# Attention scores on a head's own rows: K kept once, two units' products interleaved on two groups of rows and two banks

## What is computed

```
layer 0:  q,k of 64 per head, v of 16;  scores = (q + r_w) k^T + shifted((q + r_r) r^T);  softmax;  @ v;  @ Wo
layer 1:  q,k,v of 16 per head;          scores = q k^T / 4;   softmax;  @ v;  @ Wo     (after a gated convolution)
layer 2:  q,k,v of 64 per head;          scores = q k^T / 8;   softmax;  @ v;  @ Wo
```

## Time and profile before

| | |
|---|---|
| three runs | 1695.86, 1707.94, 1713.18 us |
| median | 1707.94 us |
| span of the profiled execution (first to last instruction) | 1698.1 us |
| median less this span | 9.8 us |
| PE busy, share of the span | 1444.5 us, 85% |
| ACT busy | 662.5 us, 39% |
| DVE busy | 683.9 us, 40% |
| POOL busy | 384.9 us, 23% |
| chain that ended last, by engine | PE 58%, issue 12%, DVE 12%, DMA 8%, ACT 6% |

### The profile page before, as it was taken

The page is one execution under the profiler, slowest core; times in us unless marked ns, Lnnn a source line. Parts: engine busy times, 40 slices in busy tenths (PEclk is TensorE's granted clock), DMA queues, the critical chain, the costliest instruction groups (busy, mean ns, idle before and its releaser), DMA issues.

```text
span 1698.1 us, 31669 instructions
## 1 busy us (share of the span) xinstructions
PE 1444.5 (85%) x10300; PEld 1049.9 (62%) x10300; DVE 683.9 (40%) x2124; ACT 662.5 (39%) x2237; POOL 384.9 (23%) x464
## 2 busy tenths in 40 slices
PE   5899986796756778888899899699999999989994
PEld 3666664632212345666678799466765776789994
DVE  5557766511101376444423622433542423551113
ACT  1667663410000233777842122153663632213331
POOL 5212222300000122222200266220220200123441
PEclk8899996587778688999998899799999999889997
DMA  8434341679998400000003366200000200126553
GB/s 219 133 83 129 82 115 28 227 242 333 311 314 249 147 1 1 1 0 0 0 0 100 107 203 197 81 1 1 0 0 0 93 37 0 30 84 199 181 175 103
DMA packets 94439, 178.73 MB, mean 105 GB/s; under 512 B 35578, under 2 KB 54168, under 8 KB 92704
## 3 DMA queue, kind: packets, MB, share of 16 engines
q1 hardware_dynamic: 80144, 130.65, 26.1%
q10 hardware_dynamic: 7056, 30.67, 5.6%
q0 software_dynamic: 7136, 16.10, 3.1%
HBM read 150.39 MB, written 26.99 MB: 104 GB/s over the span
## 4 chain that ended last, share of the span: by engine, by line
PE 58%; issue 12%; DVE 12%; DMA 8%; ACT 6%; SPq 3%; POOL 1%; DVEq 0%; ACTq 0%; POOLq 0%
PE bank L1819 15%; DMA WM<-in_fc 7%; PE bank L2339 6%; PE bank L2325 4%; PE bank L1910 4%; PE bank L1922 3%; PE bank L1939 3%; PE bank L2329 3%; PE bank L1949 3%; PE bank L2000 2%; PE bank L1885 2%; PE bank L1992 2%; ACT ON L1604 2%; SPq L226 2%; PE bank L2256 1%
## 5 line engine op out<-in xcount | busy, mean ns | idle before, releaser
L1819 PE MATMUL bank<-XT,AREA 96*128 96x408 f32 (+1 forms) x640 | 239.1, 532 | 33.9 <-ACT XT L1558 16.6
L1819 PEld LDWEIGHTS bank<-XT,AREA 96*128 96x128 f32 (+1 forms) x640 | 122.1, 196 | 139.8 <-issue 99.8
L1910 PE MATMUL bank<-KZ,QT 128*102 128x102 f32 x1152 | 140.8, 262 | 9.0 <-ACT PB L1604 5.7
L664 POOL TENSOR_TENSOR PB<-PB,RCU 102x306 f32<-102x306 f32 x96 | 69.2, 720 | 318.5 <-DVE RCU L923 318.4
L648 POOL TENSOR_TENSOR RS<-VE,expo 102x4 f32<-102x4 f32 (+1 forms) x53 | 53.0, 1001 | 387.2 <-DVE VE L863 329.8
L1910 PEld LDWEIGHTS bank<-KZ,QT 128*102 128x102 f32 x1152 | 122.4, 174 | 27.2 <-issue 18.1
L2339 PE MATMUL bank<-WM,KZ 128*128 x660 | 118.2, 327 | 0.0
L2339 PEld LDWEIGHTS bank<-WM,KZ 128*128 128x128 f32 x660 | 105.7, 190 | 0.4
L1585 ACT ACTIVATE KZ<-bank,AREA 128x128 f32<-128x128 f32 x198 | 54.6, 374 | 121.8 <-PE bank L2329 121.8
L1922 PE MATMUL bank<-AREA,OT 128*102 128x192 f32 x384 | 88.9, 345 | 11.3 <-DVE SLOTS L1276 5.3
L1939 PE MATMUL bank<-PT,V 102*32 102x102 f32 (+1 forms) x1152 | 85.9, 270 | 14.5 <-DVE OT L933 12.3
(11 more groups left out here) (335 smaller groups left out, 2777.5 us busy)
## 6 DMA issues: line engine op xcount, KB each, us to landing
AREA<-in_fc SPq DMA_DIRECT2D x10, 1536.0 KB, 26.1
SLOTS<-in_m3w SPq DMA_DIRECT2D x33, 384.0 KB
WM<-in_fc ACTq DMA_DIRECT2D x5, 2304.0 KB, 19.5
WM<-in_fc SPq DMA_DIRECT2D x6, 1536.0 KB, 27.9
AREA<-in_fc ACTq DMA_DIRECT2D x4, 2304.0 KB, 20.6
SLOTS<-in_m1w SPq DMA_DIRECT2D x33, 256.0 KB
AREA<-pos_scratch SPq DMA_DIRECT2D x16, 459.0 KB
pos_scratch<-AREA SPq DMA_DIRECT2D x8, 913.5 KB
```

Of the source, the lines that this page charges most:

```text
L664: pool.tensor_tensor(p, p, scale, ALU.mult).then_inc(sem["probs_ready"], 1)
L1819: last = pe.matmul(dst, lhsT, rhs, start=n == 0, stop=n == len(pieces) - 1)
L1910: last = pe.matmul(psum[k][0:T, cols(j)], QT[:, tile, cols(bb)], KALL[:, unit % per_tile * (HEADS // per_tile) + tile, cols(bb)], start=Tr ...
```

## The change

1. K is written once, in the layout of Q: one copy of a whole tile into KT in place of two (layers 0 and 2) or four (layer 1). The memsets, their semaphore and PE's waits for it go.
2. The score products read only their head's own rows of Q and K (64 rows, or 32 in layer 1), through `head`.
3. PE issues the scores of two units, s and s+1, together in even steps (`two_units`): by turns a product of unit s and one of unit s+1, which lie on different groups of rows and go to different banks. Both wait for their banks ahead of the first product. Each unit still signals `scores_ready` with its last product.
4. PE's order in a step changes: in an odd step projection, values, transposes; in an even step values, transposes, scores of two units, projection.
5. DVE takes the minima of both units in the even step, ahead of the reciprocals of unit s-1. ACT's and POOL's orders stay.

```diff
-                    if s < UNITS:
+                    if s < UNITS and s % 2 == 0:
                         minima(s, pos)
+                        minima(s + 1, pos)
...
-                ts(KZ[0:64, 0, p, :], src[0:64], bk0[0:64, p:p + 1], None, ALU.add)
-                free(ts(KZ[64:128, 1, p, :], src[64:128], bk0[64:128, p:p + 1], None, ALU.add), k)
+                free(ts(KT[:, p, :], src, bk0[:, p:p + 1], None, ALU.add), k)
...
-                    for u in range(UPB):
-                        rows = slice(32 * u, 32 * u + 32)
-                        last = activation(KALL[rows, 3 * u + j, :], src[rows], ACT.Identity,
-                                          bias=bqk1[rows, 3 + j:4 + j])
-                    free(last, k)
+                    free(activation(KT[:, j, :], full(k)[:, 0:TG], ACT.Identity, bias=bqk1[:, 3 + j:4 + j]), k)
...
-            pool.memset(KZ[:], 0.0).then_inc(sem["halves_cleared"], at.one("halves_cleared"))
-            pool.wait_ge(sem["halves_cleared"], at.now("halves_cleared"))
...
+                def two_units(s):
+
+                    for u in (s, s + 1):
+                        if u < len(banks):
+                            pe.wait_ge(sem[f"bank_free{banks[u]}"], at.now(f"bank_full{banks[u]}") + 1)
                         else:
                             pe.wait_ge(sem[scores_read], at.take(scores_read))
-                        for j in range(HPU):
-                            tile = unit // per_tile * HPU + j
-                            last = pe.matmul(psum[k][0:T, cols(j)], QT[:, tile, cols(bb)],
-                                             KALL[:, unit % per_tile * (HEADS // per_tile) + tile, cols(bb)],
-                                             start=True, stop=True)
-                        last.then_inc(sem["scores_ready"], at.one("scores_ready"))
+                    for j in range(HPU):
+                        for u in (s, s + 1):
+                            bb, h = u // UPB, u % UPB * HPU + j
+                            last = pe.matmul(psum[banks[u % len(banks)]][0:T, cols(j)],
+                                             head(QT, h, per_tile, 128 // per_tile, cols(bb)),
+                                             head(KT, h, per_tile, 128 // per_tile, cols(bb)), start=True, stop=True)
+                            if j == HPU - 1:
+                                last.then_inc(sem["scores_ready"], at.one("scores_ready"))
...
+                for s in range(STEPS):
+                    if s % 2:
+                        project(s)
+                    if 0 <= s - 5 < UNITS:
+                        values_of(s - 5)
+                    if 0 <= s - 3 < UNITS:
+                        turn(s - 3)
+                    if s % 2 == 0:
+                        if s < UNITS:
+                            two_units(s)
+                        project(s)
                     if pos:
                         pos(s)
```

More of the change, by code:

```diff
@@ L408, in build @@
                "second_loaded", "biases_loaded", "gelu_loaded",
[L409 removed]
+               "y_ready", *(f"y_loaded{g}" for g in range(NG)), "moe_done", "values_ready", "values_taken", "scaled",
                "attn0_done", "attn1_done",
@@ L792, in _ @@
                 pool.wait_ge(sem[f"scattered{r}"], 16 * len(range(r, TILES, YRING)))
[L793 to L796, removed]
             powers(1)
@@ L1772, in _ @@
                     k = at.bank(XBANKS)
-                    src = full(k)[:, 0:TG]
-                    activation(KZ[0:64, 0, p, :], src[0:64], ACT.Copy)
-                    free(activation(KZ[64:128, 1, p, :], src[64:128], ACT.Copy), k)
+                    free(activation(KT[:, p, :], full(k)[:, 0:TG], ACT.Copy), k)
                 attention()
@@ L1925, in attention @@
                                 filled(last, PROJBANK)
-                    n = s - 5
-                    if 0 <= n < UNITS:
-                        bb, unit = n // UPB, n % UPB
-                        f = fill_of(dv, n)
-                        k = places[f % len(places)]
-                        if n == 0:
-                            moved(*v_moved)
-                        moved(pt_moved[n])
-                        if f >= len(places) and (unit == 0 or av_filled(dv, unit - 1)):
-                            taken(f - len(places))
-                        for j in range(HPU):
-                            h = HPU * unit + j
-                            row, rows, tile, _ = av_place(dv, h)
-                            last = pe.matmul(psum[k][row:row + rows, cols(tile)],
-                                             by_head(dv)[:, bb * HEADS + h, :], PT[n % 2][:, j, :],
-                                             start=True, stop=True)
-                        if av_filled(dv, unit):
-                            last.then_inc(sem["values_ready"], 1)
@@ L1944, in attention, with values_of @@
-                    n = s - 3
-                    if 0 <= n < UNITS:
-                        pe.wait_ge(sem["probs_ready"], at.take("probs_ready"))
-                        k, p = claim(TBANKS)
-                        for j in range(HPU):
-                            last = pe.transpose(p[0:T, cols(j)], PB[n % 4][:, j, :], ident[0:T, 0:T])
-                        pt_moved[n] = filled(last, k)
+                def values_of(n):
+                    bb, unit = n // UPB, n % UPB
+                    f = fill_of(dv, n)
+                    k = places[f % len(places)]
+                    if n == 0:
+                        moved(*v_moved)
+                    moved(pt_moved[n])
+                    if f >= len(places) and (unit == 0 or av_filled(dv, unit - 1)):
+                        taken(f - len(places))
+                    for j in range(HPU):
+                        h = HPU * unit + j
+                        row, rows, tile, _ = av_place(dv, h)
+                        last = pe.matmul(psum[k][row:row + rows, cols(tile)],
+                                         by_head(dv)[:, bb * HEADS + h, :], PT[n % 2][:, j, :],
+                                         start=True, stop=True)
+                    if av_filled(dv, unit):
+                        last.then_inc(sem["values_ready"], 1)
@@ new lines, in turn @@
+                def turn(n):
+                    pe.wait_ge(sem["probs_ready"], at.take("probs_ready"))
+                    k, p = claim(TBANKS)
+                    for j in range(HPU):
+                        last = pe.transpose(p[0:T, cols(j)], PB[n % 4][:, j, :], ident[0:T, 0:T])
+                    pt_moved[n] = filled(last, k)
+                for s in range(STEPS):
[9 more added lines that the diff above has]
+                        project(s)
```

23 lines of the change are left out of this document (3 added, 20 removed).

## The result

| | before | after |
|---|---|---|
| median of the runs | 1702.3 us (4) | 1817.6 us (4, 1803.0 to 1825.9) |
| span of the profiled execution | 1698.1 us | 1824.1 us |
| mean granted clock | 0.900 | 0.816 |

What follows compares the result with a forecast made beforehand. PE was taken to bound layer 1's step at 1.29 us, ACT close at 1.26. Terms 16.8 + 8.8 + 4 - 9.2 - 3 - 4 - 1.5 + 5 = +16.9 took 1708 to 1725 us, range 1698 to 1750.

Steps and rivals of the forecast that it cites:

- The price of the products: PE's score products: two units side by side cost 0.81 us in place of 1.08, 0.27 less a pair.
- The chain through the pair: Wait loop through all four engines: 3.55 us a pair in layer 1, 3.74 in layer 2; +16.8 and +8.8 us.
- The second chain: DVE's minima, reciprocal, POOL, then PE's transposes at 3.05 us, hidden behind 3.15.
- my first rival: PE stays the bound: pairs of 2.9 us or less decide for it, 1671 us; chance 0.13.
- The clock: Layer 1's idle pairs partly at half clock, about 4.4 us a pair: +5 us, bounds 0 and +16.
- the clock falls for good: Half clock throughout the idle attentions and layer 2's beginnings: +16 in place of +5, 1740 us; chance 0.15.
- Layer 0: Attentions at 5.55 us a pair against 5.52, DVE's output copy delayed: +4 us in all, bounds -8 and +14.
- Key copies, -9.2: Layer 1's fewer key copies let scores start 2.3 us earlier a group, -9.2 us in all.
- Memsets: Removing POOL's memsets frees DVE's subtractions: -4.0 us in layer 1, -1.5 in layer 0, 0 in layer 2.
- a share of 3: Layer 0's tail, where DVE and ACT copy half as much: -3 us, bounds 0 and -6.
- Sum: All terms of the forecast together: +16.9 us on 1708, giving 1725 us.

Runs made afterwards that it cites:

- first run: Kernel before with the change's order alone, 128-row products, K's copies and memsets kept: 1800.3 us, ratio 1.057.
- sixth run: Changed kernel with ACT's copies and DVE's inverse sums ahead, scores ahead of values and transposes and the start filled in layers 1 and 2: 1782.1 us, 1.047.
- eleventh run: Kernel before with DVE's order alone changed, both units' minima ahead of the inverse sums: 1732.9 us, ratio 1.019.
- second run: Changed kernel with one unit a step and PE's and DVE's order of before, own rows and K once kept: 1893.3 us, ratio 1.115.
- twelfth: Kernel before with score products of layers 0 and 2 over 64 rows in place of 128: 1853.6 us, ratio 1.090.
- fifth run: Changed kernel with unit-matrix products filling PE only at the start of each attention in layers 1 and 2: 1799.3 us, ratio 1.054.
- tenth run: Kernel before with layer 1's score products over 32 rows, all else as before: 1790.4 us, ratio 1.051.
- seventh run: The second run's kernel with unit-matrix products filling PE at the start of each attention in layers 1 and 2: 1810.5 us, ratio 1.061.
- thirteenth: Kernel before with layers 1 and 2 taking score products over their own rows only from the seventh unit of each attention on: 1790.5 us, 1.052.
- eighth: The sixth run's kernel without the filling of the start: 1792.7 us, ratio 1.055.
- fourth run: Changed kernel with four unit-matrix products before the values of every even step, filling PE's idle time: 1849.1 us, ratio 1.088.

## Why the prediction was wrong, point by point

- **The price of the products**: right at full clock. Transposes to projection take 1.12 us with a pair between them, against 1.11 forecast and 1.39 with 128 rows (first run): the 0.27 us a pair were there. With one unit at a time, going over and back costs 0.13 us a unit (layer 1) to 0.17 (layer 2).
- **The chain through the pair**: right. 3.76 us in layer 2 against 3.74. (The second chain's links add up to 3.02 and not 3.05; nothing hangs on it.) A wait was missed beside it: with three banks a pair waits for the exponentials of the pair before, so my first rival's pair of 2.9 us or less was not to be had in layer 2 either (3.18 in the sixth run).
- **The clock**: the step that failed. I took +5 us, bounded at +16, as a lower rate on "about 20 of 56 pairs", from stretches of layer 0 after which "the clock stayed". In the changed kernel it falls at the start of every group of layers 1 and 2; it doesn't come back before the group's end in layer 1 and takes 20 us in layer 2. Beyond the chain's forecast these two layers took 62.7 - 16.8 = 45.9 and 33.7 - 8.8 = 24.9 us more; as an estimate, the clock's price there is 71 us. Two things lower the clock. The new order does so at the start of a group, where PE waits, and with 128 rows it comes back (first run). Products on 32 or 64 rows do so in before's own order and keep it down: 128 rows to 32 in layer 1 alone cost 191.9 - 112.0 = 79.9 us. I had looked for the cause in PE's idle time alone, and the earlier trace rows could not show the second. I also priced the slow pair too low at 4.4 us: 4.61 and 4.99.
- **Rival "the clock falls for good"**: the right one, at 0.15 and priced at 1740. Its price was that of the same +16, which counts 20 pairs; all 56 at 0.8 to 0.85 us would have been 45 to 48 us, and a time above the range.
- **Layer 0**: the second term that failed, +4 forecast with a bound of +14, +40.0 measured. DVE's copy behind two units' work was right as a mechanism and wrong in size: "+1 to +3.3 a group" measured 8.5 (the eleventh run), because other parts of DVE's work stand ahead of the copy too and because the clock falls after the wait. How the 40 us divide stays open: in layer 0 DVE's order alone costs 33.8 us, own rows alone 41.3 (second run) and 67.2 (twelfth).
- **Key copies, -9.2**: right at full clock, and lost to the half clock in this kernel. Layer 1's gaps from a last projection pass to the next scores are 16.9, 15.5 and 13.7 us, before 15.2 to 15.3; they begin at half clock. In the fifth run the clock is full again by then, and all three gaps are 13.1 us: 2.1 us less, forecast 2.3. Such a gap before, after the change and in the fifth run:

```profile
713.20:728.50 15.30, 12.31 (x51) 7.89 (x49) 5.45 (x19) 10.17 (x17) 1.01 (x1) 1.00 0.00 0
753.60:770.50 16.90, 16.07 (x52) 10.00 (x50) 4.87 (x17) 4.97 (x8) 1.01 (x1) 0.73 0.00 0
756.80:769.90 13.10, 12.05 (x51) 7.94 (x49) 4.87 (x17) 4.87 (x8) 1.01 (x1) 1.00 0.00 0
```

- **Memsets**: right in kind. From layer 0's last pass to layer 1's first scores it is 7.4 us less (forecast 4.0), and the first scores of layer 0 come 7.6 us earlier (forecast 1.5 and a share of 3).
- **Sum**: +62.7, +33.7, +40.0 in the attentions and -10.4 outside give the span's +126.0.

Do the parts add up? DVE's order alone is +33 us, the whole order with 128 rows +98, own rows without the order +191. The full change is +115. At half clock two units take 4.61 us in layer 1 and 4.99 in layer 2 where the second run needs 2 x 2.46 and 2 x 2.84, and in layer 2 the clock comes back 20 us after its fall where it takes 41 to 48 us in the second run. So the order takes back part of what the rows cost, and the effects don't add. That two units' products go side by side is the likely reason for the shorter pairs; no run shows it for the clock.

What stays open: by which measure of work the clock is granted. The rows of the products decide it here at equal order and equal waits, and PE's busy share in the profile does not. A rival was not tested: each unit on few rows also goes over to its group and back, and this, not the unused rows, could be what lowers the clock. Whether it is rows alone, or also that passes on different groups overlap at a start (in the tenth run PE works 2.02 of the first 3.5 us of a layer 1 attention, in the kernel before 2.62), was not told apart. Why layer 2's steady steps on 64 rows keep the clock when its starts on 64 rows lose it is the same question. Layer 1 with 64 rows in steady steps alone was not tried.

## What to carry to other kernels

Cutting a product to its own rows took nothing off its time here (six passes 0.78 us against 0.70), and can cost the clock of everything around it: before going from 128 rows to 32 or 64, look at the granted clock of a stretch that already works that way, and price the change with the slow step in the whole stage (2.46 us against 1.42), not in a few pairs. Two units at once in a pipeline over four engines close loops in which one step's slack stood before; count the banks for two pairs, not for one. And when an engine takes two steps' work in one, look at what is queued behind it from other work: that was 8.5 us a group with the clock's fall that it brought, against the 2 us of the additions and minima themselves.

## What the runs showed of the hardware that was not expected

- Score products on 32 of 128 rows: the clock fell to 0.50 from full while PE had no rest (6.00 of 6.00 us busy around the fall, seventh run), and stayed there 20 us and more with PE busy 20.00 of 20.00 (thirteenth). With 128 rows it was at full with PE at work 2.67 of 4 us (first run).
- The same products on 64 rows kept the full clock in layer 2 where the start of the group was on 128 rows (145.8 us over four groups, thirteenth run) or on 64 and filled (147.5, seventh), and lost it where the start was on 64 and not filled (226.4, twelfth).
- Filling PE with work that nothing needs helped ahead of the fall (layer 2, 165.0 to 146.9 us, eighth and sixth run; nothing in layer 1, 167.1 and 169.2) and cost time after it (fourth run).
